# Two tiled products joined on TensorE, the next batch's x split sooner, and three loads issued by ScalarE

## What is computed

```python
q = feature_map(split(x @ Wq.T + bq), orf)        # exp(proj - norm) + EPS
k = feature_map(split(x @ Wk.T + bk), orf)
v = split(x @ Wv.T + bv)
kv = jnp.einsum('nlm,nld->nmd', k, v)             # per head 128 x 32
ksum = jnp.sum(k, axis=1)
out = jnp.einsum('nlm,nmd->nld', q, concatenate([kv, ksum]))
out = out[..., :-1] / out[..., -1:]
x = layernorm(x + out @ Wo.T + bo)
x = layernorm(x + x @ ternary(W).T * scale)
```

## Time and profile before

| | |
|---|---|
| median of the runs | 1302.67 us |
| the profiled execution | 1302.63 us, of which the span is 1300.8 us |
| granted TensorE clock over the span | 0.999 of full speed |
| PE busy | 1279.1 us, 98% of the span |
| DVE, ACT, POOL busy | 73%, 54%, 29% |
| DMA | 160.56 MB, 123 GB/s on average |
| chain that ended last | PE 84%, DVE 6%, ACT 6%, issue 3% |

### The profile page before, as it was taken

How to read it: one execution, slowest core, us unless ns; L and a number is a source line. 1 busy time by engine, 2 the same in 40 slices (tenths; PEclk the granted TensorE clock), 3 DMA queues, 4 the chain that set the end, 5 groups by cost and what they waited for, 6 DMA issues and landing times.

```text
span 1300.8 us, 24924 instructions
## 1 busy us (share of the span) xinstructions
PE 1279.1 (98%) x8626; PEld 965.2 (74%) x8626; DVE 943.5 (73%) x1784; ACT 701.7 (54%) x1403; POOL 383.7 (29%) x685
## 2 busy tenths in 40 slices
PE   9999999999999999999999999999999999999986
PEld 8767787777877678776787768876688767886655
DVE  7599765886668875787657786587875788657876
ACT  5557535564355743657336663367534665446534
POOL 1213432124311343214422234212353123422143
PEclk9999999999999999999999999999999999999999
DMA  7568414773146821568215762258612686026711
GB/s 241 137 137 218 95 45 112 180 182 86 57 116 162 197 69 53 135 158 190 61 57 130 181 166 67 64 128 195 164 48 70 137 211 151 25 80 149 161 54 65
DMA packets 83773, 160.56 MB, mean 123 GB/s; under 512 B 19648, under 2 KB 37184, under 8 KB 83136
## 3 DMA queue, kind: packets, MB, share of 16 engines
q1 hardware_dynamic: 67856, 139.78, 43.5%
q10 hardware_dynamic: 9648, 16.85, 3.4%
q0 software_dynamic: 6144, 2.34, 2.1%
HBM read 39.13 MB, written 16.78 MB: 43 GB/s over the span
## 4 chain that ended last, share of the span: by engine, by line
PE 84%; DVE 6%; ACT 6%; issue 3%; DMA 1%; POOL 0%; SPq 0%; ACTq 0%; DVEq 0%; POOLq 0%
PE ps L943 28%; PE ps L980 25%; PE ps L1044 8%; PE ps L1012 4%; PE ps L966 4%; PE ps L968 4%; PE ps L967 4%; PE ps L999 4%; ACT features L687 2%; PE ps L1070 2%; ACT x_hi L655 1%; DMA rows<-in_Wk_t 1%; DVE squares_turned L853 1%; ACT unit_hi L668 0%; DVE stats L793 0%
## 5 line engine op out<-in xcount | busy, mean ns | idle before, releaser
L687 ACT ACTIVATE features<-ps 128x512 f32<-128x512 f32 x512 | 278.7, 603 | 251.7 <-PE ps L943 193.4
L584 POOL DMA_DIRECT2D stacks<-norm_rows x128 | 86.4, 681 | 306.0 <-DVE norm_rows L868 186.0
L943 PE MATMUL ps<-Wo_hi,stacks 128*128 128x512 f32 x448 | 150.4, 402 | 0.0
L660 ACT ACTIVATE values_then_attention<-ps 128x512 f32<-128x512 f32 x64 | 38.2, 597 | 196.9 <-PE ps L968 193.8
L809 DVE TENSOR_TENSOR den<-den,features 128x512 f32<-128x512 f32 x186 | 128.1, 689 | 12.9
L943 PE MATMUL ps<-orf_key_a,stacks 128*128 128x256 f32 x512 | 131.7, 288 | 0.0
L562 POOL TENSOR_SCALAR stats<-stats 128x1 f32<-128x1 f32 x128 | 36.0, 282 | 323.7 <-DVE stats L796 323.6
L943 PE MATMUL ps<-orf_key_b,stacks 68*128 68x256 f32 x512 | 128.4, 282 | 0.0
L1044 PE MATMUL ps<-features,kv_ksum 128*32 128x512 f32 x1024 | 123.1, 598 | 3.3 <-ACT features L687 2.1
L845 DVE SCALAR_TENSOR_TENSOR unit_lo<-ps,cols,unit_hi 128x512 fp32r<-128x512 f32 x128 | 94.2, 736 | 34.8 <-ACT squares L670 34.7
L943 PEld LDWEIGHTS ps<-orf_key_a,stacks 128*128 128x128 f32 x512 | 97.1, 190 | 25.8 <-issue 21.9
(11 more groups left out here) (141 smaller groups left out, 2771.4 us busy)
## 6 DMA issues: line engine op xcount, KB each, us to landing
stacks<-unit_hi SPq DMA_DIRECT2D x384, 128.0 KB, 2.4
stacks<-unit_lo SPq DMA_DIRECT2D x256, 128.0 KB, 3.8
stacks<-unit_hi SPq DMA_DIRECT2D x64, 256.0 KB, 3.8
out<-rows ACTq DMA_DIRECT2D x56, 256.0 KB, 2.0
rows<-in_x_t SPq DMA_DIRECT2D x49, 256.0 KB, 4.6
rows<-in_x SPq DMA_DIRECT2D x32, 256.0 KB, 4.4
features<-in_x SPq DMA_DIRECT2D x32, 256.0 KB, 4.4
values_then_attention<-in_x_t SPq DMA_DIRECT2D x8, 256.0 KB, 7.6
```

The lines of the kernel that those rows point to most:

```text
L584: pool.dma_start(slot[row:row + 2, c:c + L].rearrange("o (t c) -> o t c", c=DH), NN[2 * DH * p:2 * DH * (p + 1), u % 2, part, :].bitcast(F ...
L687: nc.scalar.activation(FE[:, n % 8, :, 0:M], ps[:, :].rearrange("p (a m) -> p a m", a=HG), ACT.Exp, scale=C_EXP).then_inc(a_exp.sem, 1)
L943: last = mm(out, a, b, start=(n == 0), stop=(n == len(terms) - 1))
```

## The change

It does four things.

1. *Joining.* The second GG of a group moves from the end of the query unit into the next key unit, right in front of the first four G of the next group (`deferred + half`). This is done where `joined(b, g)` holds: groups 0 to 2 of batches 0 to 6 and group 0 of the last batch, 22 places. To make room, the first part of P of units 2, 4 and 6 moves in front of their first F, half stands after the fourth F instead of the sixth, and R of the second half of the tokens moves behind the sixth F.
2. *Sooner splits.* XT is divided into the high part (`XT`, ACT) and the low part (`XO`, DVE or POOL). In unit 5 the high parts of tiles 1 and 2 come sooner. The first projection of the next batch takes its 8 products of x high first and its 4 of x low last; its first part waits for the high part alone, its second part for the low one.
3. *Loads by ACT.* The loads of tiles 5 to 7 are issued by ACT, each behind a wait for the low part of tile 0, 1 or 2, and no longer by SP.
4. *High part first.* O, OK and FF take the products of the high part first and wait for the low part only after them.

```diff
+def joined(b, g):
+    return g < (NG - 1 if b + 1 < B else 1)
...
         else:
-            seq = f(0, 1) + p[0] + f(2, 3) + p[1] + s0 + l0 + f(4, 5) + q0 + half + p[2] + early + f(6, 7) + s1 + l1 + q1 + norm + lift + p[3]
+            deferred, turned = ([("GG", b, g - 1, 1)], [("R", b, g - 1, 1)]) if joined(b, g - 1) else ([], [])
+            seq = p[0] + f(0, 1) + s0 + l0 + p[1] + f(2, 3) + deferred + half + f(4, 5) + turned + q0 + p[2] + f(6, 7) + s1 + l1 + q1 + norm + lift + p[3]
+            if b + 1 == B and u + 2 == NU:
+                seq = f(0, 1, 2, 3, 4, 5) + half + early + f(6, 7)
...
-            seq += l1 + p[3] + [("R", b, g, 0), ("GG", b, g, 1)] + q1 + norm + lift
+            seq += l1 + p[3] + [("R", b, g, 0)] + ([] if joined(b, g) else [("GG", b, g, 1), ("R", b, g, 1)]) + q1 + norm + lift
         else:
-            seq += xt(0) + kv + f(2, 3) + p[1] + [("KVT", b, g)] + s0 + l0 + xt(1, 2) + f(4, 5) + xt(3)
-            seq += [("LX", b + 1, t) for t in range(5, TT)] + p[2] + [("GG", b, g, 0), ("R", b, g, 0)] + q0
-            seq += s1 + xt(4) + f(6, 7) + xt(5) + l1 + p[3] + xt(6, 7) + [("GG", b, g, 1)] + q1 + norm + lift
+            seq += x_hi(0, 1) + x_lo(0) + kv + f(2, 3) + x_hi(2) + p[1] + [("KVT", b, g)] + x_lo(1, 2) + s0 + load(5) + l0 + f(4, 5) + load(6) + xt(3) + load(7)
+            seq += p[2] + [("GG", b, g, 0)] + s1 + l1
+            seq += [("R", b, g, 0)] + q0 + xt(4) + f(6, 7) + xt(5) + p[3] + xt(6, 7) + q1 + norm + lift
...
+                elif kind == "LX" and u > 4:
+                    act.wait_ge(*x_split(b, u - 5))
+                    act.dma_start(x_stage(b, u), xt_tiles[b, u]).then_inc(d_xl[u].sem, 16)
...
-                    if u == 0 and part == 0:
+                    if u == 0 and part == 0 and b:
+                        pe.wait_ge(a_xhi.sem, a_xhi.nth(b, 4 * h + 4))
+                    elif u == 0 and part == int(b > 0):
                         pe.wait_ge(*x_split(b, 4 * h + 3))
...
+                    if b and u == 0:
+                        terms = [t for n, t in enumerate(terms) if n % 3 < 2] + terms[2::3]
```

More of the change, by code:

```diff
@@ L85, in xt, with x_hi, load, x_lo @@
     def xt(*tiles):
+        return [s for t in tiles for s in x_hi(t) + x_lo(t)]
+    def x_hi(*tiles):
         return [("XT", b + 1, t) for t in tiles] if b + 1 < B else []
+    def load(t):
+        return [("LX", b + 1, t)] if b + 1 < B else []
+    def x_lo(*tiles):
+        return [("XO", b + 1, t) for t in tiles] if b + 1 < B else []
     two, three = later(2), later(3)
@@ L118, in unit_stages @@
             seq += kv + f(2, 3) + p[1] + [("KVT", b, g)] + s0 + l0 + f(4, 5) + p[2] + f(6, 7) + s1 + q0 + [("GG", b, g, 0)]
-            seq += l1 + p[3] + [("R", b, g, 0), ("GG", b, g, 1)] + q1 + norm + lift
+            seq += l1 + p[3] + [("R", b, g, 0)] + ([] if joined(b, g) else [("GG", b, g, 1), ("R", b, g, 1)]) + q1 + norm + lift
         else:
-            seq += xt(0) + kv + f(2, 3) + p[1] + [("KVT", b, g)] + s0 + l0 + xt(1, 2) + f(4, 5) + xt(3)
-            seq += [("LX", b + 1, t) for t in range(5, TT)] + p[2] + [("GG", b, g, 0), ("R", b, g, 0)] + q0
-            seq += s1 + xt(4) + f(6, 7) + xt(5) + l1 + p[3] + xt(6, 7) + [("GG", b, g, 1)] + q1 + norm + lift
+            seq += x_hi(0, 1) + x_lo(0) + kv + f(2, 3) + x_hi(2) + p[1] + [("KVT", b, g)] + x_lo(1, 2) + s0 + load(5) + l0 + f(4, 5) + load(6) + xt(3) + load(7)
+            seq += p[2] + [("GG", b, g, 0)] + s1 + l1
+            seq += [("R", b, g, 0)] + q0 + xt(4) + f(6, 7) + xt(5) + p[3] + xt(6, 7) + q1 + norm + lift
             seq += [("LR", b, t) for t in range(4)]
-        seq += [("R", b, g, 1)] if b + 1 < B or u < NU - 3 else []
         if u == 1 and b == 0:
@@ L186, in first @@
 def first(kind, *tiles):
-    return [(kind, 0, t) for t in tiles]
+    return [stage for t in tiles for stage in [(kind, 0, t)] + [("XO", 0, t)] * (kind == "XT")]
 PROLOGUE = [("W", 0, 0, 0), ("W", 0, 0, 1)] + first("XT", 0) + [("W", 0, 0, 2), ("W", 0, 0, 3)] + first("LW", 1)
@@ L482, in _ @@
                     else:
-                        wait(*x_split(b, t - 5))
+                        continue
                     load_x(b, t)
@@ L595, in _ @@
                     lift_norms(b, t)
-                elif kind == "XT" and b and t >= 4:
+                elif kind == "XO" and b and t >= 4:
                     c = slice(P * t, P * (t + 1))
@@ L834, in _ @@
                     ternary(u)
-                elif kind == "XT" and (b == 0 or u < 4):
+                elif kind == "XO" and (b == 0 or u < 4):
                     dve.wait_ge(a_xhi.sem, a_xhi.nth(b, u + 1))
@@ L1047, in _ @@
                 elif kind == "O":
-                    pe.wait_ge(v_alo.sem, v_alo.nth(b, u + 1))
+                    pe.wait_ge(a_ahi.sem, a_ahi.nth(b, u + 1))
                     if b == 0 and u == 0:
@@ L1052, in _ @@
                     al = ST[:, 1, 1024 + D * (u % 2):1024 + D * (u % 2 + 1)]
-                    terms = [t for k in range(KT) for t in (
-                        (ah[:, P * k:P * (k + 1)], WH["o"][:, k, :]), (ah[:, P * k:P * (k + 1)], WL["o"][:, k, :]),
-                        (al[:, P * k:P * (k + 1)], WH["o"][:, k, :]))]
-                    products(ps[:, :], terms).then_inc(t_o.sem, 1)
+                    for n, (k, w) in enumerate((k, w) for k in range(KT) for w in (WH["o"], WL["o"])):
+                        mm(ps[:, :], ah[:, P * k:P * (k + 1)], w[:, k, :], start=(n == 0), stop=False)
+                    pe.wait_ge(v_alo.sem, v_alo.nth(b, u + 1))
+                    for k in range(KT):
+                        last = mm(ps[:, :], al[:, P * k:P * (k + 1)], WH["o"][:, k, :], start=False, stop=(k == KT - 1))
+                    last.then_inc(t_o.sem, 1)
                 elif kind == "OK":
@@ L1059, in _ @@
                     part = (k, u // 4) if k < NG - 1 else (k, u // 4, u % 4 // 2)
-                    pe.wait_ge(v_glo.sem, v_glo.nth(0, groups.index(part) + 1))
+                    pe.wait_ge(a_ghi.sem, a_ghi.nth(0, groups.index(part) + 1))
                     a_hi, a_lo = (X[:, u, P * k:P * (k + 1)] for X in (last_hi, last_lo))
@@ L1063, in _ @@
                     mm(ps[:, :], a_hi, WL["o"][:, k, :], start=False, stop=False)
+                    pe.wait_ge(v_glo.sem, v_glo.nth(0, groups.index(part) + 1))
                     last = mm(ps[:, :], a_lo, WH["o"][:, k, :], start=False, stop=(k == KT - 1))
@@ L1074, in _ @@
                         pe.wait_ge(s_tern, KT)
+                    hi, lo = turned_rows(b, u)
+                    pe.wait_ge(a_yhi.sem, a_yhi.nth(b, u + 1))
+                    for k in range(KT):
+                        mm(ps[:, :], hi[:, P * k:P * (k + 1)], WT3[:, k, :], start=(k == 0), stop=False)
                     pe.wait_ge(v_ylo.sem, v_ylo.nth(b, u + 1))
-                    hi, lo = turned_rows(b, u)
-                    terms = [(part[:, P * k:P * (k + 1)], WT3[:, k, :]) for k in range(KT) for part in (hi, lo)]
-                    products(ps[:, :], terms).then_inc(t_ff.sem, 1)
+                    for k in range(KT):
+                        last = mm(ps[:, :], lo[:, P * k:P * (k + 1)], WT3[:, k, :], start=False, stop=(k == KT - 1))
+                    last.then_inc(t_ff.sem, 1)
 def kernel(**inputs):
```

## The result

The changed kernel takes 1306.84 us (median of 20 runs, 1302.45 to 1318.72), the kernel before, run on the same chips, 1302.64 (20 runs, 1301.43 to 1306.03). The ratio is 1.0043, 95% interval 1.0031 to 1.0055: slower by 4 to 7 us, where 6.8 us faster was forecast. The profiled execution took 1305.79 us with a span of 1303.9. I read the same views as before.

A forecast was written before the change was run, and what follows sets the result against it. PE, busy for 98% of the span, was taken as the bound. 1302.63 - 6.8 (joins) - 5.6 (waits that go) + 5.6 (new wait) = 1295.8 us; 8 in 10 range 1290.5 to 1303.

The forecast's parts named there:

- Part 1: Joining GG to the next unit's G saves one visit to tiled products: 0.31 us at 22 joins, 6.8 us.
- What the join moves: Shifts around the joined GG on PE, ACT and DVE: costed at nothing, else up to 0.5 us at 22 places.
- Part 3: At P for tiles 4 to 7, PE newly waits for x_hi of tile 7: 0.8 us a batch, 5.6 lost.
- Part 2: Around unit 5's end, waits for x_lo and the last exponential go: 0.80 us in seven batches, 5.6 us.
- Part 4: High part first in O and FF changes nothing: 0, with 0 to 1 us as bounds for the tail.
- A: ACT's loads of tiles 5 to 7 land early, new x_hi wait about 0.1 us: 1290.9 us; chance 0.18.
- D: Joins don't pay: the seam costs 0.31 us or DVE's additions return it at the sums: 1302.6 us; chance 0.08.
- B: Loads as slow as before, whoever issues them, x_hi wait 2.0 us: 1304.2 us, or 1302.1; chance 0.14.
- C: Slower: ACT waits for DVE's x_lo before each load, x_hi wait 2.7 us: 1309.1 us; chance 0.08.

The follow-up runs named there:

- the last experiment but one: Kernel before with 15 joins, R behind the norm steps, and the next x's first projection taking high parts first: 1297.52 us, ratio 0.9958.
- the first experiment: Changed kernel, but SP again issues the loads of x tiles 5 to 7, behind its lifts: 1305.15 us, ratio 1.0006.
- the loads truly later: Changed kernel, with ACT's three loads behind tile 3's x_hi and held until that step is done: 1310.16 us, ratio 1.0053.

## Why the prediction was wrong

**Part 1, the joins: right in mechanism, 0.355 us a join instead of 0.31.** That is measured at 14 places in units 1 to 4; for all 22 it would be 7.8 us. The seam between GG and G is free, as rows 5 had it: GG takes 1.74 us in front of G. The Trainium skill ("TensorE: Matmul & The Clock Gate", What overlaps and what doesn't) says that a weight load overlaps with products in flight only when its row group differs; by that rule the seam would cost time, and the 1.74 us, 0.11 less than in front of a plain product, speak against it for column tiles.

**The step that failed is in part 1 too: "What the join moves".** I followed the joined GG on PE, its exponential on ACT and its additions on DVE, and costed the rest at nothing. I did not ask what had been hidden behind the second GG on PE's side: the DMA that brings the norms for the next unit's F. The same gap is in part 3, which lets PE pass "two key F" of unit 6 in 0.96 us without asking whether their rows are there. In batch 2 the lifts had 2.2 us of air. The third join and the sooner x order took 1.4 of it from PE's side, the join before it (of group 1, in unit 4) 1.2 from DVE's, and the slower landing beside the new loads 2.6 more. In the sum, the 5.6 us for waits stand against 13.7 us by which unit 5 is longer than 11.08 (its length with no loads) in seven batches, and 3.1 us of half clock in unit 6 of batches 2 and 3. None of my rivals had this place, so the range, built from them, ended at 1303, 3.8 us under the time.

**Part 2, the waits that go: they went**, 1.0 us a batch with the third join where no load was in flight, 1.11 worked out (0.80 and 0.31). But they go only because GG moves away as well. With GG left where it was, the time comes back at its exponential: it starts at 10.65 or 10.66 us of unit 5 in the kernel before, in the changed kernel without the third join, and in the last experiment but one.

**Part 3, the wait for x_hi of tile 7: not seen in the changed kernel**, hidden behind the longer one. It is there as soon as the norm wait is not: 0.6 to 2.9 us a batch in the first experiment. In the changed kernel x_hi of tile 7 is itself late, in batch 2 by ACT's timeline:

```profile
436.72 0.63 ACT L671 ACTIVATE x_hi<-rows 128x512 fp32r<-128x512 f32 x1 [0.62 <-DMA rows<-in_x_t]
```

It ends 14.3 us after the start of unit 5, and in the mean of seven batches at 13.2, where PE with timely lifts would ask at 12.05 (11.09 and two key F of 0.96). So timely lifts alone would have left a wait of about 1.15 us (an estimate from these starts) where I had priced 0.8. Two readings under it were off and in part cancelled. The third load did not go out behind the high part of tile 3, at 7.7 to 8.5 us of unit 5 as I worked out, but at 5.84, before that step began. And my landing was too hopeful: 2.0 us for ACT's stores says nothing for a stretch with a DMA share near 1, where the same kind of issue took 4.0 to 7.8. (ACT is free at 433.60 + 1.15 = 434.75 by the earlier trace rows, not at 434.6; that changes nothing here.)

**Part 4: 0, confirmed** in its experiment (0.9993). **Rivals.** A fell by the landing times; D by the seam. B was right that the loads come as late as before, whoever issues them: the third goes out about 1.7 us sooner, but lands 12.6 us after the start of unit 5 in the mean of seven batches, 12.9 before. Only, this was not what PE waited for longest. The Trainium skill ("Trainium Kernel Development and Optimization", Key Constraints) says that issuing from several engines saves only the sequencer's issue time; for the loads themselves these times agree, and the sooner moment shows in the lifts beside them. C's sign was right, its place was not: ACT's x_hi steps up to tile 4 start at the same distance from unit 5's start with and without the loads (8.84 us for tile 4).

Left open: how much of the slower landing is the 16 engines' full load and how much the order in which they serve three queues; no run here separates them. The share alone does not tell: it is 0.99 from 427 to 437 us both before and after. The times of the changed kernel spread over 16 us, and the longest go with the lowest mean clock (0.987 at 1318.72, 0.998 at 1302.45). That the half clock behind a wait makes this spread is likely from batches 2 and 3 above, but is not shown: there is one profile of this kernel.

## What to carry to other kernels

Before work is moved off a stretch, list every transfer that has its deadline in it, not only the one that the edit speaks of, and write down when it lands, when it is needed, and how far each edit shifts either; here the air was 2.2 us and three shifts, each small, asked for 5.2. A load that is issued sooner can slow whoever is in flight then, small transfers too, and may itself land hardly sooner: ask whose deadline falls into the time until it lands, up to 8 us here. Take joins of tiled products where no deadline stands behind them, and the gain holds: 15 of the 22, with the norms kept early, made the kernel 5 us faster.

## What the runs showed of the hardware

- ACT issues a DMA ahead of activations that stand before it in its row, 1.3 us ahead in the rows above, and the activations around it keep their starts (8.84 us for tile 4's x_hi with the loads and without). It cost ACT time, 1.4 us for three, where the issues had to wait for the activation just before them to end.
- An 8 KB lift in unit 5 lands in 3.1 to 4.3 us with no x loads in flight (seven batches), in 4.2 to 7.8 in the changed kernel, with three of 256 KB issued beside it by ACT. Held back by 3 us or more, the same loads leave it at 3.1 to 4.1.
- Soon after 2.9 us of standing still PE's granted clock was 0.50 for 3.4 us, at a price of about 1.5 us more. The length of the stop alone does not decide it: with the loads truly later it followed stops of 1.5 us in batches 2 and 6 and not one of 2.8 in batch 1.
- Between GG's and G's tiled products, both on 128 rows but of other shapes and operands, no time is lost: GG takes 1.74 us there, 1.85 in front of a plain product.
